# Attention and expert kernel: the transposition of the next block's rows moved from TensorE to VectorE and on-chip transfers

## The reference, cut

```python
x = x + xattn(layernorm(x), ctx, Wq, bq, Wk, bk, Wv, bv, W1, b1, W2, b2)
#   q = ln(x) @ Wq + bq; scores, softmax, @ v;  h = relu(out @ W1 + b1);  h @ W2 + b2
x = x + ffn(layernorm(x), Wg, ln_scale, ln_bias, W1e, b1e, W2e, b2e)
#   top1 = argmax(xt @ Wg.T);  xhat = normalised xt
#   h = gelu((xhat * s_e + b_e) @ w1_e + bb1_e);  y = h @ w2_e + bb2_e  for e = top1
```

## Time and profile before

| | us |
|---|---|
| median of 3 runs | 1406.38 |
| profiled execution | 1402.3 |
| its span | 1400.3 |
| granted TensorE clock, mean | 0.999 |
| PE busy | 1382.0 |
| DVE busy | 991.0 |
| ACT busy | 612.0 |
| POOL busy | 334.0 |

### The profile page before, as it was taken

How to read it: one execution, slowest core, us unless ns; L and a number is a source line. 1 busy time by engine, 2 the same in 40 slices (tenths; PEclk the granted TensorE clock), 3 DMA queues, 4 the chain that set the end, 5 groups by cost and what they waited for, 6 DMA issues and landing times.

```text
span 1400.3 us, 23958 instructions
## 1 busy us (share of the span) xinstructions
PE 1382.0 (99%) x8590; PEld 1039.6 (74%) x8590; DVE 991.0 (71%) x2073; ACT 612.0 (44%) x1146; POOL 334.0 (24%) x293
## 2 busy tenths in 40 slices
PE   8999999999999999999999999999999999999998
PEld 5486868677776868686867777686868686788897
DVE  6667676686767676777767676767676766649887
ACT  4534334443424343534434342524243343448886
POOL 2311212021111212121201111121212120108887
PEclk9999999999999999999999999999999999999999
DMA  7200302021120303130212102020202021458885
GB/s 293 75 30 1 91 1 77 31 88 46 40 89 24 104 3 99 36 98 31 84 46 68 61 31 84 6 91 1 91 1 91 1 61 61 158 182 266 295 261 178
DMA packets 56916, 118.16 MB, mean 84 GB/s; under 512 B 8329, under 2 KB 16786, under 8 KB 55906
## 3 DMA queue, kind: packets, MB, share of 16 engines
q1 hardware_dynamic: 46002, 82.93, 19.2%
q0 software_dynamic: 10800, 33.70, 6.3%
HBM read 73.77 MB, written 44.66 MB: 85 GB/s over the span
## 4 chain that ended last, share of the span: by engine, by line
PE 96%; DVE 2%; issue 1%; POOL 1%; DMA 0%; ACT 0%; POOLq 0%; SPq 0%; DVEq 0%; ACTq 0%
PE bank L1176 25%; PE bank L1220 13%; PE bank L1200 12%; PE bank L1011 12%; PE bank L1099 8%; PE bank L1081 5%; PE bank L1601 4%; PE bank L1639 3%; PE bank L1036 3%; PE bank L1262 2%; PE bank L979 2%; PE bank L1585 2%; PE bank L1280 1%; PE bank L1055 1%; PE bank L883 1%
## 5 line engine op out<-in xcount | busy, mean ns | idle before, releaser
L1176 PE MATMUL bank<-actA,w 128*128 128x512 f32 x1536 | 368.8, 395 | 1.4 <-DVE actA L1147 1.4
L1176 PEld LDWEIGHTS bank<-actA,w 128*128 128x128 f32 x1536 | 282.4, 188 | 63.5 <-issue 5.6
L1089 ACT ACTIVATE E<-bank 77x512 f32<-77x512 f32 x256 | 132.3, 591 | 170.1 <-PE bank L1081 170.1
L1220 PE MATMUL bank<-w,actH 128*128 128x512 f32 x768 | 195.6, 400 | 0.0
L1200 PE MATMUL bank<-w,actH 128*128 128x512 f32 x768 | 184.8, 393 | 0.0
L1011 PE MATMUL bank<-actA,wq 128*128 128x512 f32 x768 | 182.7, 390 | 0.0
L1049 DVE TENSOR_REDUCE mx<-bank 128x4 f32<-128x308 f32 x256 | 104.6, 472 | 101.1 <-PE bank L1036 101.1
L1220 PEld LDWEIGHTS bank<-w,actH 128*128 128x128 f32 x768 | 138.6, 188 | 44.5 <-issue 18.3
L1011 PEld LDWEIGHTS bank<-actA,wq 128*128 128x128 f32 x768 | 142.7, 188 | 28.2 <-issue 0.5
L1200 PEld LDWEIGHTS bank<-w,actH 128*128 128x128 f32 x768 | 142.0, 188 | 28.2
L1185 ACT ACTIVATE actH<-bank,b 128x512 fp32r<-128x512 f32 x128 | 88.2, 689 | 161.8 <-PE bank L1176 160.2
(11 more groups left out here) (179 smaller groups left out, 1911.1 us busy)
## 6 DMA issues: line engine op xcount, KB each, us to landing
rowB<-region SPq DMA_DIRECT2D x71, 258.0 KB, 3.8
xn<-in_x SPq DMA_DIRECT2D x64, 256.0 KB, 2.8
rows<-in_x SPq DMA_DIRECT2D x64, 256.0 KB, 3.3
w_raw<-in_W SPq DMA_DIRECT2D x2, 2048.0 KB, 11.8
e_raw<-in_E SPq DMA_DIRECT2D x16, 256.0 KB, 2.8
region<-padrow SPq DMA_DIRECT2D x9, 258.0 KB, 4.2
e_parts<-e_high SPq DMA_DIRECT2D x8, 256.0 KB, 2.0
e_parts<-e_low SPq DMA_DIRECT2D x8, 256.0 KB, 2.3
```

The source lines that it names most:

```text
L1089: act.activation(E[0:M, g % 2, h, :], of("ST", b, g, h)[0:M, :], ACT.Exp).then_inc(S["act_exp"], 1)
L1176: mm = pe.matmul(p[:], w, a, start=k == 0 and j == 0, stop=k == KD - 1 and j == 2)
L1220: mm = pe.matmul(p[:], actH[:, ha, m, P * s:P * s + P], w2[:, hw, m, :], start=n == 0, stop=n == 23)
```

## The change

For blocks 2 to 15 (`DT` = 2) PE no longer transposes. The rows of a block are loaded in another order (`"(t s j) d -> s t j d"`). At the end of the XSTAT chain DVE makes four transposes, each of one whole `xn[s]` (128x512, in squares of 32x32) into `xq`, which lies over the low half of `actQ`. SP then issues sixteen transfers of 32 rows of 2 KB each (XTD), which put the rows into place in `xn[0]` to `xn[3]`. XTS takes XT's place: ACT and DVE make the high and low half of `actA` as before, from `xn` instead of a bank, and ACT waits for the transfers and for H.

To make room, XSTAT of block b+1 moves to the start of the H stage (from m = 3 or 4), X2STAT of block b-1 to m = 4, or 6 where an expert is prepared (from the start, or m = 1), RK and SCAT and the loads of `rows` to m = 6 (from 5), E1_ACC to m = 4, behind a DRAIN (from the start), E1_SUM and E1_CENTER and its store to m = 6 (from 2). The loads of `xn` are issued before m = 0. `e1_raw` lies over `mT` and `e1_acc` over `att`, so E1_RAW waits for all scores of block b+1 (`pe_s`) and the first MTOUT of the block after for the store.

```diff
+DT = 2
...
-    xn = [sb(f"xn{i}", [P, D]) for i in range(SUB)]
+    xn_all, xn_at = sb("xn", [P, SUB, D])
+    xn = [xn_all[:, i, :] for i in range(SUB)]
...
+    xq = at("xq", [P, HG, KD, SUB, HD], F32, actQ_at + 4 * KD * BLK)
...
-    e1_raw = at("e1_raw", [P, KD, EH], F32, xn_at + 8 * D)
-    e1_acc = at("e1_acc", [P, 2, EH], F32, xn_at + 12 * D)
+    e1_raw = at("e1_raw", [P, KD, EH], F32, mT_at)
+    e1_acc = at("e1_acc", [P, 2, EH], F32, att_at)
...
             if last:
                 step("TAB_LOAD")
                 step("EB_LOAD")
+            else:
+                step("XNLOAD", b + 1, 2)
+                step("XNLOAD", b + 1, 0)
             prep = b - 1 - PREP0 if PREP0 < b <= PREP0 + NE else None
-            if prep is not None:
-                step("E1_ACC", prep)
-            elif b:
+            if last:
                 step("X2STAT", b - 1)
                 step("DRIP", 8)
+            elif b:
+                step("XSTAT", b + 1)
+                step("DRIP", 8)
             logits = 2
-            ranks = 4 if last else 5
+            ranks = 4 if last else 6
             for m in range(MF):
                 if m >= 2:
                     step("H", b, m)
                 step("HHI", b, m)
-                if prep is not None and m == 2:
+                if prep is not None and m == 6:
                     step("E1_SUM", prep)
...
-                if prep is not None and m == 1:
-                    step("X2STAT", b - 1)
                 if m:
                     step("DRIP", 6)
-                if not last and m == 0:
-                    step("XNLOAD", b + 1, 0)
-                if not last and m == 0 and prep is None:
-                    step("XNLOAD", b + 1, 2)
                 if context is not None and m == 0:
                     step("VLOAD", context)
-                if not last and m == 3 and prep is not None:
-                    step("XNLOAD", b + 1, 2)
-                if prep is not None and m == 2:
+                if b and m == logits + 1:
+                    step("OH", b - 1)
+                if b and m == (3 if last else 4):
+                    step("DRAIN")
+                    if not last:
+                        step("XTD", b + 1)
+                        if prep is not None:
+                            step("E1_ACC", prep)
+                if prep is not None and m == 6:
                     step("E1_CENTER", prep)
                     step("E1_STORE", prep)
-                if b and m == 3:
-                    step("DRAIN")
-                if b and m == logits + 1:
-                    step("OH", b - 1)
+                if b and not last and m == (4 if prep is None else 6):
+                    step("X2STAT", b - 1)
...
-                if m == (3 if prep is None else 4) and not last:
+                if m == 3 and b == 0:
                     step("XSTAT", b + 1)
...
                 for s in range(2):
-                    step("XT", b + 1, s)
+                    step("XTS" if b + 1 >= DT else "XT", b + 1, s)
                 step("YA", b, 1)
                 for s in range(2, SUB):
-                    step("XT", b + 1, s)
+                    step("XTS" if b + 1 >= DT else "XT", b + 1, s)
...
         def sp_xnload(sp, b, s0):
             for s in (s0, s0 + 1):
-                if b:
-                    sp.wait_ge(S["pe_xT"], SUB * (b - 1) + s + 1)
                 if b == 1:
+                    sp.wait_ge(S["pe_xT"], s + 1)
                     sp.wait_ge(st_v, 16 * (NB - 1))
-                if PREP0 + 2 <= b < PREP0 + 2 + NE:
-                    if s0:
-                        sp.wait_ge(st_e1, 16 * (b - PREP0 - 1))
-                    else:
-                        sp.wait_ge(st_e2, 32 * (b - PREP0 - 1))
+                elif b:
+                    sp.wait_ge(S["dve_xT"], SUB * b)
+                if PREP0 + 2 <= b < PREP0 + 2 + NE and s0 == 0:
+                    sp.wait_ge(st_e2, 32 * (b - PREP0 - 1))
+                x = A["x"][b * BLK:b * BLK + BLK, :]
+                if b >= DT:
+                    x = x.rearrange("(t s j) d -> s t j d", s=SUB, j=HD)[s]
+                else:
+                    x = x[P * s:P * s + P]
+                sp.dma_start(xn[s], x).then_inc(ld_xn[s], 16)
...
         def sp_e1raw(sp, e):
-            sp.wait_ge(S["pe_xT"], SUB * (PREP0 + e + 2))
+            sp.wait_ge(S["pe_s"], KD * (PREP0 + e + 2))
...
         def sp_e2raw(sp, e):
-            sp.wait_ge(S["pe_xT"], SUB * (PREP0 + e + 2))
+            sp.wait_ge(S["dve_xT"], SUB * (PREP0 + e + 2))
...
+                if b >= DT:
+                    dve.wait_ge(S["pe_s"], KD * b)
+                    for s in range(SUB):
+                        dve.wait_ge(S["dve_xn"], SUB * b + s + 1)
+                        dve.transpose(xq[:, :, :, s, :], xn[s].rearrange("p (k f j) -> p f k j", k=KD, j=HD)
+                                      ).then_inc(S["dve_xnT"], 1)
+                        yield
             chains.append(chain())
...
+        def sp_xtd(sp, b):
+            sp.wait_ge(S["dve_xnT"], SUB * (b - DT + 1))
+            for t in range(SUB):
+                for f in range(HG):
+                    sp.dma_start(xn[t][HD * f:HD * f + HD], xq[HD * t:HD * t + HD, f].rearrange("p k s j -> p (k s j)")
+                                 ).then_inc(ld_xT[t], 16)
+
+        def act_xts(act, b, t):
+            act.wait_ge(ld_xT[t], 16 * HG * (b - DT + 1))
+            act.wait_ge(S["pe_h"], MF * b)
+            act.activation(actA[:, 0, :, P * t:P * t + P], xn[t].rearrange("p (k t) -> p k t", k=KD), ACT.Identity
+                           ).then_inc(S["act_xT"], 1)
+
+        def dve_xts(dve, b, t):
+            if t == 0:
+                drain()
+            dve.wait_ge(S["act_xT"], SUB * b + t + 1)
+            dve.tensor_tensor(actA[:, 1, :, P * t:P * t + P], xn[t].rearrange("p (k t) -> p k t", k=KD),
+                              f32(actA[:, 0, :, P * t:P * t + P]), ALU.subtract).then_inc(S["dve_xT"], 1)
...
         def act_mt(act, b, pr):
+            if PREP0 + 2 <= b < PREP0 + 2 + NE and pr == 0:
+                act.wait_ge(st_e1, 16 * (b - PREP0 - 1))
...
         def dve_e1acc(dve, e):
             dve.wait_ge(L["e1raw"], 16 * (e + 1))
+            dve.wait_ge(S["pool_o"], (KD - 1) * (PREP0 + e + 2))
```

More of the change, by code:

```diff
@@ L99, in xattn_moe_kernel @@
     mx, _ = sb("mx", [P, SUB, P])
-    mT, _ = sb("mT", [P, BLK], F32R)
+    mT, mT_at = sb("mT", [P, BLK], F32R)
     sel, _ = sb("sel", [P, 2, KS], F32R)
     one, _ = sb("one", [P, HD])
-    att, _ = sb("att", [P, BLK])
+    att, att_at = sb("att", [P, BLK])
     wg, _ = sb("wg", [P, KD, HD])
@@ L108, in xattn_moe_kernel @@
     csb, _ = sb("csb", [P, BLK])
-    xn = [sb(f"xn{i}", [P, D]) for i in range(SUB)]
-    xn_at = xn[0][1]
-    xn = [t[0] for t in xn]
+    xn_all, xn_at = sb("xn", [P, SUB, D])
+    xn = [xn_all[:, i, :] for i in range(SUB)]
     b2bc, _ = sb("b2bc", [P, D])
@@ L240, in xattn_moe_kernel @@
         ld_x = [[sem(f"ld_x{i}_{s}") for s in range(SUB)] for i in range(2)]
+        ld_xT = [sem(f"ld_xT{t}") for t in range(SUB)]
         st_v, ld_v = sem("st_v"), sem("ld_v")
@@ L250, in xattn_moe_kernel @@
             "act_wq dve_wq act_w1 pool_w1 act_w2 dve_w2 act_kbd dve_sel dve_tri "
-            "dve_xn pool_xb pe_xT act_xT dve_xT pe_q act_q dve_q pe_sm dve_max pe_mt act_mt pe_s act_exp "
+            "dve_xn dve_xnT pool_xb pe_xT act_xT dve_xT pe_q act_q dve_q pe_sm dve_max pe_mt act_mt pe_s act_exp "
             "pe_sums dve_rc pe_av dve_n act_o pool_o dve_o pe_h act_h dve_h pe_y dve_x2 dve_row pool_ones pe_gate dve_gate "
@@ L693, in sp_xnload @@
             for s in (s0, s0 + 1):
-                if b:
-                    sp.wait_ge(S["pe_xT"], SUB * (b - 1) + s + 1)
                 if b == 1:
+                    sp.wait_ge(S["pe_xT"], s + 1)
                     sp.wait_ge(st_v, 16 * (NB - 1))
-                if PREP0 + 2 <= b < PREP0 + 2 + NE:
-                    if s0:
-                        sp.wait_ge(st_e1, 16 * (b - PREP0 - 1))
-                    else:
-                        sp.wait_ge(st_e2, 32 * (b - PREP0 - 1))
-                sp.dma_start(xn[s][:], A["x"][b * BLK + P * s:b * BLK + P * s + P, :]).then_inc(ld_xn[s], 16)
+                elif b:
[8 more added lines that the diff above has]
+                sp.dma_start(xn[s], x).then_inc(ld_xn[s], 16)
         def sp_xload(sp, b):
@@ L756, in sp_tabload @@
         def sp_tabload(sp):
-            sp.wait_ge(S["pe_xT"], SUB * NBLK)
+            sp.wait_ge(S["dve_xT"], SUB * NBLK)
             sp.dma_start(jt[:], A["jt"][:, 0:N1, :]).then_inc(L["jt"], 16)
@@ L1718, in xattn_moe_kernel @@
             "XT": {"pe": pe_xT, "act": act_xT, "dve": dve_xT},
+            "XTD": {"sp": sp_xtd},
+            "XTS": {"act": act_xts, "dve": dve_xts},
             "XB": {"pool": pool_xb},
```

## The result

The changed kernel takes 1439.3 us (median of 4 runs) against 1406.93 of the kernel before (4 runs beside it): a ratio of 1.023, interval 1.0212 to 1.0248. The forecast was 1398.9, and the range of the prediction went from 1384 to 1413.

What follows compares the result with a forecast made beforehand. PE was taken as the bound everywhere. Gains of 6 x 1.74 less losses of 8 x (2.0 + 0.1 - 1.74) gave 10.4 - 2.9 = 7.5 us, so 1406.4 - 7.5 = 1398.9 us, range 1384 to 1413.

Steps and rivals of the forecast that it cites:

- The gain: XT on PE in blocks 2 to 15: two pairs of 0.87 us a block go, 1.74 each, 24.4 us in all.
- The price of a DVE transpose: DVE's 128x512 transposes: taken as 0.69 us each, 0.62 as they overlap, with bounds 0.48 and 1.24.
- the rival that made it dear: DVE transposes cost up to 1.24 us, PE waits at E1_SUM and before Q, change slower: 1425 us; chance 0.17.
- the prediction's own sign: PE's waits on DVE's e_acc: 8 times about 2 us expected; above 3 us each, the transpose is dear.
- the upper bound of 1.24 us: DVE transpose at its dearest, after a 128x512 operation of 1244 ns: E1_SUM's wait would be 4.5 us.
- SP's queue: Order of SP's transfers: xn loads land at 589.3, before DVE wants them at 592.1; E2_RAW hidden, narrowly; cost 0.
- the 2.0 forecast: PE at E1_SUM waits for DVE's e_acc from 609.45 to about 611.4, 2.0 us, in 8 blocks.
- the sum's own form: Whole kernel: 6 x 1.74 gained, less 8 x (2.0 + 0.1 - 1.74) lost, 7.5 us faster.
- Behind E1_SUM: DVE after H7 drains X2STAT and makes XTS's low halves before PE wants Q; just fits, 0.1 us charged.
- The sixteen transfers: SP's XTD: sixteen issues take 7.7 us, land 2.3 later at 617.7 to 618.2, hidden before XTS; cost 0.
- E2_RAW: Load behind XLOAD in SP's queue: lands near 633.5, ACT waits 1 to 2 us, hidden, narrowly.
- The third rival: The sixteen transfers come late before Q, at 1 us an issue 3.5 us late in 6 blocks: 1432; chance 0.07.

Runs made afterwards that it cites:

- b_best: Changed kernel with loads of xn cut into eight transfers, E1_SUM at m = 7, E1_CENTER and its store behind the low halves of XTS: 1379.85 us, ratio 0.9828.
- a_loads: Changed kernel with only the loads of xn for blocks 2 to 15 cut into eight transfers of 32 whole partitions: 1389.1 us, ratio 0.9905.
- a_busy: Changed kernel with only 20 extra PE matmuls before the wait at E1_SUM, in the 8 blocks that prepare an expert: 1413.85 us, ratio 1.0084.
- a_sum7: Changed kernel with only E1_SUM, E1_CENTER and its store moved from m = 6 to m = 7, loads left late: 1404.18 us, ratio 1.0008.
- b_order: Kernel before, with only the rows of blocks 2 to 15 loaded in the changed order (four groups of 32), not put back: 1402.99 us, ratio 0.9993.
- b_order8: Kernel before, with the rows of blocks 2 to 15 loaded in eight groups of 16, not put back: 1403.59 us, ratio 1.0001.

## Why the prediction was wrong, point by point

**The gain** held: blocks without an expert went from 75.77 to 73.95 us, 1.81 each for the 1.74 of the working. In b_best nearly all of it was measured, 23.9 us over the 14 blocks.

**The price of a DVE transpose** held, and with it fell the rival that made it dear. The groups of DVE, to set beside the earlier trace rows:

```profile
L987 DVE STREAM_TRANSPOSE xq<-xn 128x512 f32<-128x512 f32 x56 | 37.5, 691 | 0.0
L1019 DVE TENSOR_TENSOR actA<-xn,actA 128x512 fp32r<-128x512 f32 x56 | 35.0, 682 | 0.7 <-issue 0.4 <-ACT actA L1012 0.2
```

691 ns alone, and 0.60 to 0.62 us as they follow each other (1.21 for two, from 625.93 to 627.14). By the prediction's own sign a wait above 3 us meant a dear transpose; the wait was 4.5 and the transpose was not dear, far from the upper bound of 1.24 us. The low halves from SBUF take 682, as taken from e_low.

**The step that failed** is in "SP's queue": "Two store issues (1 us), 2.3 to land, two issues and 2.8 to land: 589.3, before DVE wants them at 592.1." The landing time was taken from a load of whole contiguous parts, and the change loads in another order, which the working mentioned nowhere. The queue was nearly right: with the 17.9 us taken off, the last load was issued at 587.4, and the sum above has it at 586.5. (It left out the issue of E1_RAW, 0.6 us, and the store landed after 3.2 us instead of 2.3.) What was far off is the landing: 11.9 us after the issue (605.31 to 617.19) for 2.8, so at 599.3 instead of 589.3. DVE's statistics were 6.5 us late (ended at 601.6 for 595.1), of which the waits for ACT and LT took up a part, and E1_SUM came at 4.5 instead of 2.0. With the loads recut (a_loads) the same sum can be read clean: 1.36 us of wait for the 2.0 forecast, and 1389.1 against 1403.3, a gain of 14.2 for the 7.5 forecast. By the sum's own form that is 6 x 1.81 + 8 x (1.81 - 1.36) = 14.5. The Trainium skill would have given it ("DMA: Bandwidth & Descriptors", section "Why a DMA increments its semaphore by 16 and not by 1"): a transfer runs on the largest number of engines up to 16 that divides the size of the slowest dimension on both sides. The slowest dimension of the new source is 4. By that rule a load runs on 4 engines, a share of 0.25, and with 8 groups on 8, a share of 0.5; both are estimates. The runs agree: 0.26, and 0.44 to 0.50.

**The term that was missing** is the clock. The working charged a wait of PE at its length alone. Measured, a wait of 4.5 us costs 2.7 to 2.9 us more (a_busy), because PE then runs H7 at the lower level; a wait of 1.36 us cost nothing more (a_loads: 2.84 for H7). The granted clock stood at 1.00 in all of the earlier trace rows, so these rows don't show the price. But the end of the trace before shows that the clock falls behind an idle PE. PE's last matmul begins at 1394.35 and takes 0.40 us; then:

```profile
1397.00:1398.00 1.00, 0.00 (x0) 0.00 (x0) 0.00 (x0) 0.00 (x0) 0.74 (x1) 0.60 0.04 1
1398.00:1399.00 1.00, 0.00 (x0) 0.00 (x0) 0.00 (x0) 0.00 (x0) 0.24 (x1) 0.50 0.04 1
```

The Trainium skill ("TensorE: Matmul & The Clock Gate", section "Part 1: The HAM clock gate (the "warmup" mystery)") states that the throttled level of 1.2 GHz is the default and that activity of PE releases it. The traces agree: 0.50 behind the idle stretches here, 1.00 in the same place where PE was kept busy.

The two together: 8 blocks at 81.85 - 76.26 = 5.6 us more are 45 us, less 6 x 1.81 = 11, is 34; measured are 32.4 between the medians. (The two traces differ by 37.4; 3.8 of it lie outside these blocks, and why is open.) Of the 5.6, 4.54 are the wait, 2.7 to 2.9 the clock, less the 1.81 of the transposes; that makes 5.4 to 5.6.

**Behind E1_SUM** held: DVE drained X2STAT and made the low halves until 648.5, and PE began Q at 649.2. It was tight, with 0.7 us to spare.

**The sixteen transfers** were mis-sized but stayed hidden. An issue takes 10.10/16 = 0.63 us, not 0.48, and they land after 2.0 (median); they overlap, so the 32 us of a row without overlap did not come. ACT waits for them, nearly only in the blocks without an expert; PE doesn't. **E2_RAW** came late for ACT by 2.8 us on average, hidden as well:

```profile
ACT actA L1012 <- DMA xn<-xq: 26.9, 16, 3.0
ACT e_high L1434 <- DMA e_raw<-in_E: 19.8, 7, 3.6
```

**The third rival** gave 1432, near the measured time by chance, and is still wrong: the transfers that came late were the loads of `xn`, not the sixteen. Its place, Q, has no wait.

## What to carry to other kernels

When a change reorders a load, its landing time is a new number: look at the outermost dimension that the transfer is left with before taking a time from a row of the old one. When a change lets TensorE wait where it did not, charge a wait of some 2 us or more at more than its length (here 2.7 to 2.9 us on top of 4.5, and in five blocks of eight 1.2 to 1.6 on top of waits of 1.75 to 2.8), and test it by filling the wait with idle matmuls. And move a short operation of a full engine behind the one that the bound engine waits for: here moving the 1.3 us of E1_CENTER was worth 6.5 us in the sum of the 8 blocks' lengths (ratio 0.9883 to 0.9828, in runs beside different runs of the kernel before).

## What the runs showed of the hardware that was not expected

- 20 extra matmuls in place of each long wait (a_busy) made the kernel 22 us faster than the same kernel without them: the granted clock stayed at 1.00 where it had been 0.50.
- The same 256 KB landed in 2.8 us (median) in contiguous order and kept a share of 0.75 of the DMA engines busy for two loads at a time; in four groups the share was 0.26 (b_order), in eight 0.44 (b_order8).
- Waits of about 2 us (a_sum7) were not told apart by their length: the clock fell behind one of 1.75 us and not behind one of 2.02, and H7 took 4.59 us or 3.02. The runs of this kernel spread over 12 us where others spread over 1 to 6.
